# First stage of a graph recurrent kernel: each matmul of 500 columns issued as two of 250 columns

## The chip, the cores and the metric

The kernel runs on one core of a Trainium2 chip. The metric is the device time of one execution in microseconds. A core has a tensor engine (TensorE, "PE" in the profile, whose weight loads are listed apart as "PEld"), VectorE (DVE), ScalarE (ACT), GpSimd (POOL), and SyncE (SP), which here only issues DMAs. The engines run their own instruction streams and meet at semaphores.

## The reference, cut to what matters

With B = 2048 samples, N = 50 nodes, D = 32 features and T = 2 maskers, the part that the change touches is the first:

```
fusion = x.reshape(b, n * d)                                        # 2048 x 1600
adj = jnp.einsum('bn,tnm->btm', fusion, masker_param) + masker_bias # 2048 x 2 x 2500
adj = jax.nn.relu(adj).reshape(b, t, n, n)
adj = adj / (adj.sum(axis=-1, keepdims=True) + 1e-06)
```

After it come one graph recurrence step with adj (gates, sigmoid, tanh), a batch norm, a layer norm, attention scores with a softmax, and a weighted sum to the output of 2048 x 64.

## The kernel before, in words

Three stages run one after the other; only the first is changed. It computes adj, normalised and turned, and stores it to DRAM as adjT; the second stage (lines 674 to 716 on TensorE) does the recurrence, the third (lines 1149 to 1233) the norms and the attention.

In the first stage the product has the samples of a tile (128) as rows of the output, and the 5000 adjacency entries are cut into 10 groups of 500 columns (`GW`), each being 10 rows (`GN`) of 50. The outer loop goes over 2 blocks of 8 sample tiles, the next over the 10 groups, and the innermost over the 8 tiles of the block: 2 x 10 x 8 = 160 windows, numbered c. Even and odd windows (c2 = 0 and 1) use different buffers. The contraction of 1600 features (with the bias as a further row) takes 13 chunks of up to 128 rows.

Products are in the type fp32r. Each operand is split in a high part, its cast to fp32r, and a low part, the remainder (`x_hi`, `x_lo`, `w_hi`, `w_lo`), and three products (low x high, high x low, high x high) are added up in PSUM for each of the first 12 chunks; the last chunk needs two. So a window has 12 x 3 + 2 = 38 matmuls, the stationary operand being 128 columns of x, the moving one 500 columns of w, all accumulated into one PSUM bank (`mm_out(c2)`, bank 0 or 1). In the notation of the profile the second name of a row is the stationary operand: in "psum<-w_hi,x_lo" x_lo is loaded and w_hi streams.

In the middle of a window (after the chunks of unit `T_AT` = 3, so 24 matmuls in) TensorE does four transposes (line 321) of the window before, which wait for VectorE's `an_ready`. ScalarE does relu (line 229) from the finished bank into `u`, and later the copy of the transposed tile (line 235); VectorE does row sums, an addition, a reciprocal and a multiplication (lines 276 to 284) into `an`. At the last window of a group ScalarE and VectorE also split the next group's w (lines 210 and 216). A window's first matmul waits for `u_ready` of the window two before (its bank is then free). SyncE issues the loads of x and w and the store of each tile. PSUM has 8 banks of 512 fp32 a partition (`BANK` = 512); the first stage uses banks 0 and 1 for products, 2 and 3 for transposes.

Of the kernel before, what the change touches and what calls it, by code (L numbers as in the profile page):

```python
# [18 lines left out]
ACT = mybir.ActivationFunctionType  # L19
# [7 lines left out]
KF = KX // P  # L27
# [8 lines left out]
GW = GN * N  # L36
# [5 lines left out]
RK = 125  # L42
# [13 lines left out]
BANK = 512  # L56
# [27 lines left out]
def stage1(nc, psum, xT, W, adjT, ident_d):  # L84
    with ExitStack() as ctx:
# [9 lines left out]
        u = sb("u", [P, 2, GN, N])  # L95
# [8 lines left out]
        mm_done, u_ready, an_ready = sem("mm_done"), sem("u_ready"), sem("an_ready")  # L104
        tr_done, at_ready = sem("tr_done"), sem("at_ready")
        at_stored = [sem("at_stored0"), sem("at_stored1")]
        dve_step = sem("dve_step")

        def mm_out(c2):

            return psum[:, c2 * BANK:c2 * BANK + GW]

        def tr_out(c2):

            return psum[0:RK, (2 + c2) * BANK:(3 + c2) * BANK]

        block = ctx.enter_context(nc.Block())

# [55 lines left out]
        def split_x_hi(act, bt, half):  # L174
            act.wait_ge(x_loaded[half], 16 * (bt + 1))
            if bt >= BLK and half == 0:

                act.wait_ge(mm_done, (GROUPS - 1) * BLK + bt - BLK + 1)
            cols = bass.ts(bt % BLK, P)
            if half == 0:  # L180
                nc.scalar.copy(x_hi[:, 0:XH, cols], x_raw[:, 0:XH, :]).then_inc(x_hi_ready, 1)
            else:
                nc.scalar.copy(x_hi[:, XH:KF, cols], x_raw[:, XH:KF, :])
                nc.scalar.copy(x_hi[0:KLAST, KF, cols], x_raw[0:KLAST, KC, :])
                nc.scalar.copy(x_lo[:, KF, cols], x_raw[:, KF, :]).then_inc(x_hi_ready, 1)
# [12 lines left out]
        def split_w_hi(act, i, it):  # L198

            act.wait_ge(w_loaded[i], (it + 1) * 16)  # L200
            if not (isinstance(it, int) and it == 0):

                if i == NU - 1:
                    act.wait_ge(mm_done, it * BLK)
                else:
                    act.wait_ge(w_used, (it - 1) * (NU - 1) + i + 1)
            k0, k1 = UNITS[i]
            if i == NU - 1:
                nc.scalar.copy(w_lo[0:KLAST, KF, :], w_raw[0:KLAST, KC, :])
            nc.scalar.copy(w_hi[:, k0:k1, :], w_raw[:, k0:k1, :]).then_inc(w_hi_ready, 1)  # L210
# [12 lines left out]
        @block.scalar  # L223
        def _(act):
            def relu(c, c2, start=False):
                act.wait_ge(mm_done, c + 1)
                if not start:
                    act.wait_ge(an_ready, c - 1)
                nc.scalar.activation(u[:, c2].rearrange("p n m -> p (n m)"), mm_out(c2), ACT.Relu).then_inc(u_ready, 1)  # L229

            def evacuate(c, c2, start=False):
                act.wait_ge(tr_done, c + 1)
                if not start:
                    act.wait_ge(at_stored[c2], 8 * (c - c2))
                nc.scalar.copy(at[:, c2].rearrange("p k b -> p (k b)"), tr_out(c2)).then_inc(at_ready, 1)  # L235

            split_x_hi(act, 0, 0)
            for i in range(NU):
                split_w_hi(act, i, 0)
                if i == 0:  # L240
                    split_x_hi(act, 0, 1)
            for blk in range(BLOCKS):
                for it, group in p1_iters(act, blk):
                    static = isinstance(it, int)
                    for w in range(BLK):
                        c = it * BLK + w
                        split = w == BLK - 1 and not (static and it == ITERS - 1)
                        if not (static and it == 0 and w == 0):
                            relu(c - 1, (w - 1) % 2, start=static and it == 0 and w <= 2)
                        if static and it == GROUPS and w == 0:  # L250
                            for half in range(2):
                                split_x_hi(act, 2 * BLK - 1, half)
                        if static and it == 0 and w + 1 < BLK:
                            for half in range(2):
                                split_x_hi(act, w + 1, half)
                        if split:
                            for i in range(0, T_AT + 1):
                                split_w_hi(act, i, it + 1)
                        if not (static and it == 0 and w == 0):
                            evacuate(c - 1, (w - 1) % 2, start=static and it == 0 and w <= 2)  # L260
                        if split:
                            for i in range(T_AT + 1, NU):
                                split_w_hi(act, i, it + 1)
                        if static and it == GROUPS - 1 and w >= 1:
                            for half in range(2):
                                split_x_hi(act, BLK + w - 1, half)
            c = ITERS * BLK - 1
            relu(c, 1)
            evacuate(c, 1)

# [42 lines left out]
        @block.tensor  # L313
        def _(pe):
            def transposes(c, c2, start=False):
                pe.wait_ge(an_ready, c + 1)
                if not start:
                    pe.wait_ge(at_ready, c - 1)
                flat = an[:, c2].rearrange("p n m -> p (n m)")
                for k in range(AK):  # L320
                    last = nc.tensor.transpose(tr_out(c2)[:, k * P:(k + 1) * P], flat[:, k * RK:(k + 1) * RK], ident[:, :])  # L321
                last.then_inc(tr_done, 1)

            def window(it, w, blk, c, start=False, bank_free=False, none_before=False):
                pe.wait_ge(x_ready, 2 * (blk * BLK + w) + 1)
                if not bank_free:
                    pe.wait_ge(u_ready, c - 1)
                cols = bass.ts(w, P)
                for i, (k0, k1) in enumerate(UNITS):
                    if i == X_UNIT:  # L330
                        pe.wait_ge(x_ready, 2 * (blk * BLK + w) + 2)
                    if w == 0:
                        pe.wait_ge(w_ready, it * NU + i + 1)
                    for k in range(k0, k1):
                        if k < KF:
                            products = ((x_lo, w_hi, P), (x_hi, w_lo, P), (x_hi, w_hi, P))
                        else:
                            products = ((x_lo, w_hi, P), (x_hi, w_lo, KLAST))
                        for n, (a, b, r) in enumerate(products):
                            last = nc.tensor.matmul(mm_out(w % 2), a[0:r, k, cols], b[0:r, k, :],  # L340
                                                    start=k == 0 and n == 0, stop=k == KF and n == 1)
                    if i == NU - 1:
                        last.then_inc(mm_done, 1)
                    elif w == BLK - 1:
                        last.then_inc(w_used, 1)
                    if none_before and i == NU - 1:
                        pe.wait_ge(ident_loaded, 16)
                    if i == T_AT and not none_before:
                        transposes(c - 1, (w - 1) % 2, start=start)

            for blk in range(BLOCKS):
                for it, group in pe_iters(pe, blk):
                    static = isinstance(it, int)
                    for w in range(BLK):
                        c = it * BLK + w
                        window(it, w, blk, c, start=static and it == 0 and w <= 2,
                               bank_free=static and it == 0 and w < 2, none_before=static and it == 0 and w == 0)
            transposes(ITERS * BLK - 1, 1)

def p1_iters(eng, blk):

    base = blk * GROUPS
    yield base, 0
    with eng.Fori(1, GROUPS - 1) as g:
        yield base + g, g
    yield base + GROUPS - 1, GROUPS - 1

def pe_iters(eng, blk):  # L370

    base = blk * GROUPS
    if blk == 0:
        yield 0, 0
    with eng.Fori(1 if blk == 0 else 0, GROUPS) as g:
        yield base + g, g
# [979 lines left out]
```

## Time and profile before

| | |
|---|---|
| median of 2 runs | 2315.03 us (2314.99 to 2315.07) |
| profiled execution, its own time | 2318.24 us |
| its span, first to last instruction | 2316.5 us |
| mean granted TensorE clock | 0.973 of full speed |
| TensorE busy (matmuls) | 2198.9 us, 95% |
| weight loads busy | 1737.8 us, 75% |
| VectorE, ScalarE, GpSimd busy | 1091.0, 962.2 and 136.2 us |

The profiled execution is 1.74 us longer than its span and 3.21 us longer than the median of the runs. The busy time of overlapping matmuls is counted once, and a matmul's recorded length holds its passage through the array as well, so that consecutive ones overlap. What an instruction costs TensorE is therefore read from the distance between the starts of two neighbours, not from the length of one.

### The profile page before, as it was taken

To read this page: it belongs to the slowest core of one execution; us is meant where nothing else is said; L and a number is where in the kernel's file an instruction comes from. 1 tells how busy PE (TensorE), PEld (TensorE's weight loads), DVE (VectorE), ACT (ScalarE), POOL (GpSimd) and SP (SyncE) were. 2 spreads that over 40 slices of the span, in tenths; PEclk is the share of its full clock that TensorE was granted. 3 is DMA by queue.
4 is the path that set the end of the run, shared out by engine and by line. 5 is a ranking of instruction groups with operands and counts; after the bars stand their busy time and mean duration, and the time that the engine had idled before them with its cause. 6 is when DMAs were issued, how large, how long until landed. Compare 5 with 4: busy or idle time off the path is not lost. (4 is left out here: it accounts for less than half of the span.)

```text
span 2316.5 us, 34741 instructions
## 1 busy us (share of the span) xinstructions
PE 2198.9 (95%) x12302; PEld 1737.8 (75%) x12302; DVE 1091.0 (47%) x2177; ACT 962.2 (42%) x1637; POOL 136.2 (6%) x124
## 2 busy tenths in 40 slices
PE   8999999999999999999999999299999999975888
PEld 7888888888888888888888888277777777752333
DVE  4433233332345223333233332178888888873656
ACT  4322122221234212222122221088888988865551
POOL 0000000000000000000000000011101111104340
PEclk9999999999999999999999999699999999986899
DMA  6421222212234222221222211577777677619440
GB/s 208 151 75 44 88 91 90 74 45 88 92 128 143 64 90 90 91 69 50 89 90 91 72 48 27 124 171 184 186 201 181 188 199 181 181 65 261 122 119 5
DMA packets 341744, 264.06 MB, mean 114 GB/s; under 512 B 169334, under 2 KB 302998, under 8 KB 339990
## 3 DMA queue, kind: packets, MB, share of 16 engines
q1 hardware_dynamic: 323546, 225.69, 34.5%
q10 hardware_dynamic: 18144, 37.69, 5.0%
q8 instruction: 29, 0.48, 0.1%
q14 instruction: 25, 0.20, 0.0%
HBM read 195.65 MB, written 67.70 MB: 114 GB/s over the span
## 5 line engine op out<-in xcount | busy, mean ns | idle before, releaser
L340 PE MATMUL psum<-w_hi,x_lo 128*128 128x500 f32 x2080 | 823.0, 396 | 8.6 <-DVE w_lo L216 8.6
L340 PE MATMUL psum<-w_lo,x_hi 128*128 128x500 f32 (+1 forms) x2080 | 811.0, 390 | 0.0
L340 PE MATMUL psum<-w_hi,x_hi 128*128 128x500 f32 x1920 | 745.1, 388 | 0.0
L276 DVE TENSOR_REDUCE rows<-u 128x10 f32<-128x500 f32 x160 | 107.7, 673 | 893.5 <-ACT u L229 892.8
L340 PEld LDWEIGHTS psum<-w_hi,x_lo 128*128 128x128 f32 x2080 | 392.1, 188 | 84.4 <-issue 7.9
L340 PEld LDWEIGHTS psum<-w_lo,x_hi 128*128 128x128 f32 (+1 forms) x2080 | 392.5, 189 | 73.2
L340 PEld LDWEIGHTS psum<-w_hi,x_hi 128*128 128x128 f32 x1920 | 361.7, 188 | 72.9
L235 ACT COPY at<-psum 125x512 f32<-125x512 f32 x160 | 93.8, 586 | 677.4 <-PE psum L321 677.4
L229 ACT ACTIVATE u<-psum 128x500 f32<-128x500 f32 x160 | 94.1, 588 | 342.4 <-PE psum L340 342.3
L674 PE MATMUL psum<-adj_sb,xs_sb 100*64 100x100 f32 x2048 | 200.6, 350 | 30.1 <-DMA xs_sb<-xz 30.1
L674 PEld LDWEIGHTS psum<-adj_sb,xs_sb 100*64 100x64 f32 x2048 | 144.4, 149 | 73.9 <-issue 63.7
L652 POOL TENSOR_TENSOR xg_lo<-xg_sb,xg_hi 128x400 fp32r<-128x400 f32 x64 | 67.1, 1049 | 1961.4 <-ACT xg_hi L486 1961.4
L520 ACT ACTIVATE r_gate<-psum,bias 64x400 f32<-64x400 f32 x256 | 151.2, 591 | 18.3 <-PE psum L699 15.8
L216 DVE TENSOR_TENSOR w_lo<-w_raw,w_hi 128x1000 fp32r<-128x1000 f32 x120 | 144.1, 1201 | 23.6 <-ACT w_hi L210 17.4
L210 ACT CAST w_hi<-w_raw 128x1000 fp32r<-128x1000 f32 (+1 forms) x140 | 135.6, 969 | 46.3 <-PE psum L340 45.0
L525 ACT ACTIVATE psum<-psum,bias 64x400 f32<-64x400 f32 x256 | 142.3, 556 | 12.7 <-DVE hG L595 6.9
L284 DVE TENSOR_TENSOR an<-u,rows 128x500 f32<-128x500 f32 x160 | 108.8, 680 | 6.9
L603 DVE BATCH_NORM_STATS2 stats<-hC 128x128 f32 (+1 forms) x400 | 88.7, 282 | 49.3 <-ACT hC L498 48.9
L321 PEld LDWEIGHTS psum<-ident_sb,an 128*125 128x125 f32 x640 | 94.1, 186 | 17.8 <-DVE an L284 3.2
L321 PE MATMUL psum<-ident_sb,an 128*125 128x128 f32 x640 | 96.0, 272 | 4.0 <-DVE an L284 4.0
L1013 DVE SCALAR_TENSOR_TENSOR pr<-h,nmu_sb,psum 128x512 f32<-128x512 f32 x100 | 70.5, 743 | 47.0 <-PE psum L1221 24.6
L570 DVE TENSOR_TENSOR m_lo<-psum,m_hi 128x400 fp32r<-128x400 f32 x128 | 70.6, 552 | 28.6 <-ACT m_hi L490 28.6
(160 smaller groups left out, 2284.8 us busy)
## 6 DMA issues: line engine op xcount, KB each, us to landing
w_raw<-W SPq DMA_DIRECT2D x140, 500.0 KB, 7.9
adjT<-at SPq DMA_DIRECT2D x160, 250.0 KB
adj_sb<-adjT SPq DMA_DIRECT2D x32, 1250.0 KB
xs_sb<-xz SPq DMA_DIRECT2D x16, 1600.0 KB
hF<-hC ACTq DMA_DIRECT2D x96, 256.0 KB, 6.7
h<-hF SPq DMA_DIRECT2D x64, 256.0 KB, 4.5
xg_sb<-xg ACTq DMA_DIRECT2D x14, 800.0 KB, 8.0
h<-hF SPq DMA_DIRECT2D x48, 192.0 KB, 3.7
```

What stands on the lines that cost most here:

```text
L210: nc.scalar.copy(w_hi[:, k0:k1, :], w_raw[:, k0:k1, :]).then_inc(w_hi_ready, 1)
L216: nc.vector.tensor_tensor(w_lo[:, k0:k1, :], w_raw[:, k0:k1, :], w_hi[:, k0:k1, :].bitcast(fp32), ALU.subtract).then_inc(w_ready, 1)
L229: nc.scalar.activation(u[:, c2].rearrange("p n m -> p (n m)"), mm_out(c2), ACT.Relu).then_inc(u_ready, 1)
L235: nc.scalar.copy(at[:, c2].rearrange("p k b -> p (k b)"), tr_out(c2)).then_inc(at_ready, 1)
L276: nc.vector.tensor_reduce(rows[:, 0], u[:, c2], AX.X, ALU.add).then_inc(dve_step, 1)
L284: nc.vector.tensor_tensor(an[:, c2], u[:, c2], rows[:, 2].unsqueeze(2).to_broadcast([P, GN, N]), ALU.mult).then_inc(an_ready, 1)
L321: last = nc.tensor.transpose(tr_out(c2)[:, k * P:(k + 1) * P], flat[:, k * RK:(k + 1) * RK], ident[:, :])
L340: last = nc.tensor.matmul(mm_out(w % 2), a[0:r, k, cols], b[0:r, k, :], start=k == 0 and n == 0, stop=k == KF and n == 1)
L520: last = nc.scalar.activation(r_gate[half], rz_bank(pair)[half], ACT.Sigmoid, bias=bias[half, R_G:R_G + 1])
L525: last = nc.scalar.activation(z_bank[half], rz_bank(pair)[other], ACT.Sigmoid, bias=bias[other, Z_G:Z_G + 1])
L603: last = nc.vector.bn_stats(stats[:, bass.ds(tile, 1), c, :].rearrange("p i v -> p (i v)"), hC[:, c, :])
L674: last = nc.tensor.matmul(out_[SH * i:SH * i + SH, :, gi], xs[:, r, b, :], adj[:, r, :, b], start=True, stop=True)
```

## The change: two halves into two banks

Each of the 38 products of a window is issued as two matmuls with the same stationary operand, one for columns 0 to 249 and one for 250 to 499 of w. They write the first 250 columns of two neighbouring banks. `mm_out(c2)` becomes a view of both banks, `[P, 2, 250]`, and relu reads it in one instruction. Products take banks 0 to 3, transposes move to banks 4 and 5. The semaphores, their counts and the order of everything else are as before.

```diff
+        HW = GW // 2
+
+        def mm_half(c2, part):
+
+            return psum[:, (2 * c2 + part) * BANK:(2 * c2 + part) * BANK + HW]
+
         def mm_out(c2):
 
-            return psum[:, c2 * BANK:c2 * BANK + GW]
+            return psum[:, 2 * c2 * BANK:(2 * c2 + 2) * BANK].rearrange("p (h n) -> p h n", h=2)[:, :, 0:HW]
 
         def tr_out(c2):
 
-            return psum[0:RK, (2 + c2) * BANK:(3 + c2) * BANK]
+            return psum[0:RK, (4 + c2) * BANK:(5 + c2) * BANK]
...
-                nc.scalar.activation(u[:, c2].rearrange("p n m -> p (n m)"), mm_out(c2), ACT.Relu).then_inc(u_ready, 1)
+                nc.scalar.activation(u[:, c2].rearrange("p (h n) m -> p h (n m)", h=2), mm_out(c2), ACT.Relu).then_inc(u_ready, 1)
...
                         for n, (a, b, r) in enumerate(products):
-                            last = nc.tensor.matmul(mm_out(w % 2), a[0:r, k, cols], b[0:r, k, :],
-                                                    start=k == 0 and n == 0, stop=k == KF and n == 1)
+                            for part in range(2):
+                                last = nc.tensor.matmul(mm_half(w % 2, part), a[0:r, k, cols], b[0:r, k, part * HW:part * HW + HW],
+                                                        start=k == 0 and n == 0, stop=k == KF and n == 1)
```

## Rows read from the trace of the kernel before

**Rows 1.** The page: span, busy time of each engine, granted TensorE clock in 40 slices.

```profile
span 2316.5 us, 34741 instructions
PE 2198.9 (95%) x12302; PEld 1737.8 (75%) x12302; DVE 1091.0 (47%) x2177; ACT 962.2 (42%) x1637; POOL 136.2 (6%) x124
...
PEclk9999999999999999999999999699999999986899
```

**Rows 2.** Busy by stretch: length, PE, PEld, DVE, ACT, POOL, clock, DMA, GB/s.

```profile
300.00:500.00 200.00, 200.00 (x931) 167.73 (x930) 56.91 (x106) 42.77 (x64) 0.00 (x0) 1.00 0.25 82
...
1600.00:2000.00 400.00, 399.98 (x3389) 316.84 (x3386) 346.83 (x785) 354.81 (x673) 48.35 (x46) 1.00 0.73 189
```

**Rows 3.** The one line 229, relu: durations, first and last start, what it waits for.

```profile
L229 ACT ACTIVATE u<-psum x160: 576/588/592, 21.5 to 1460.1; 128x500 f32<-128x500 f32 x160
...
  PE psum L340: 342.3, 139
```

**Rows 4.** Timeline of one window: start, length (us), engine, line.

```profile
500.35 0.39 PE L340 MATMUL psum<-w_hi,x_lo 128*128 128x500 f32 x1
...
502.33 0.68 DVE L284 TENSOR_TENSOR an<-u,rows 128x500 f32<-128x500 f32 x1
...
505.52 0.39 PE L340 MATMUL psum<-w_hi,x_hi 128*128 128x500 f32 x1
505.75 0.60 PE L321 MATMUL psum<-ident_sb,an 128*125 128x128 f32 x4
...
506.11 0.48 PE L340 MATMUL psum<-w_hi,x_lo 128*128 128x500 f32 x1
...
506.42 0.39 PE L340 MATMUL psum<-w_lo,x_hi 128*128 128x500 f32 x1
```

**Rows 5.** The page, costliest groups, line 340: busy us, mean ns, idle before.

```profile
L340 PE MATMUL psum<-w_hi,x_lo 128*128 128x500 f32 x2080 | 823.0, 396 | 8.6 <-DVE w_lo L216 8.6
L340 PE MATMUL psum<-w_lo,x_hi 128*128 128x500 f32 (+1 forms) x2080 | 811.0, 390 | 0.0
L340 PE MATMUL psum<-w_hi,x_hi 128*128 128x500 f32 x1920 | 745.1, 388 | 0.0
...
L340 PEld LDWEIGHTS psum<-w_hi,x_lo 128*128 128x128 f32 x2080 | 392.1, 188 | 84.4 <-issue 7.9
L340 PEld LDWEIGHTS psum<-w_lo,x_hi 128*128 128x128 f32 (+1 forms) x2080 | 392.5, 189 | 73.2
L340 PEld LDWEIGHTS psum<-w_hi,x_hi 128*128 128x128 f32 x1920 | 361.7, 188 | 72.9
```

**Rows 6.** The one line 321, transposes: durations ns min/median/max.

```profile
L321 PE MATMUL psum<-ident_sb,an x640: 270/272/374, 26.7 to 1463.0; 128*125 128x128 f32 x160
```

**Rows 7.** Timeline of the third stage: loads and matmuls of 512 columns.

```profile
2211.23 0.19 PEld L1208 LDWEIGHTS psum<-w_lo,spread_sb 100*128 100x128 f32 x1 [0.84 <-issue]
...
2211.34 0.19 PEld L1209 LDWEIGHTS psum<-w_hi,spread_sb 100*128 100x128 f32 x1
...
2211.57 0.39 PE L1209 MATMUL psum<-w_hi,spread_sb 100*128 100x512 f32 x1
...
2211.81 0.39 PE L1208 MATMUL psum<-w_lo,spread_sb 100*128 100x512 f32 x1
...
2212.97 0.40 PE L1209 MATMUL psum<-w_hi,spread_sb 100*128 100x512 f32 x1
```

**Rows 8.** Timeline of the second stage: four intervals of 400 columns.

```profile
1962.14 0.34 PE L705 MATMUL psum<-m_lo,wd_hi 128*128 128x400 f32 x1
...
1962.87 0.35 PE L705 MATMUL psum<-xg_hi,wd_hi 128*128 128x400 f32 x1
```

**Rows 9.** Instructions of ScalarE by line and shape, first stage.

```profile
L181 ACT CAST x_hi<-x_raw 128x1024 fp32r<-128x1024 f32 x10 | 10.5, 1050 | 17.1 <-DMA x_raw<-xT 14.6 <-PE psum L340 2.6
...
L185 ACT CAST x_lo<-x_raw 128x128 fp32r<-128x128 f32 x10 | 3.0, 297 | 0.0
```

**Rows 10.** Timeline of the second stage: plain fp32 matmuls of 100 columns.

```profile
1963.15 1.57 PE L674 MATMUL psum<-adj_sb,xs_sb 100*64 100x100 f32 x16
```

## The prediction, made before the change was built

> **What bounds the kernel now.** I read the page first, for how full the engines are: the span is 2316.5 us, TensorE has matmuls in 95% of it, and its granted clock is full (2.4 GHz) in every slice of the first 1400 us [rows 1]. Busy time by stretch comes next, for where that is true: from 300 to 500 us TensorE is busy in 200.00 of 200.00 us, VectorE in 56.91 and ScalarE in 42.77 [rows 2]. The first stage is bound by TensorE alone, and the others have three quarters of their time free. Third, the group of relu: its 160 runs start between 21.5 and 1460.1 us, and ScalarE mostly waits for the product of line 340 before one (342.3 us in 139 waits) [rows 3]. So 159 windows take 1438.6 us, which is 9.048 us a window, and whatever a window costs TensorE more or less goes to the end time 160 times. The later stages are not touched; they start when the last tile is stored.
>
> Last, the timeline of one window, for what TensorE pays per instruction. The transposes take it from 505.75 to 506.11, 0.36 us, and the matmul after them 0.31 us where others take 0.225, 0.085 more [rows 4]. That leaves 9.048 - 0.445 = 8.603 us for 38 products: **226.4 ns for a load and 500 columns**. Taken directly from the timeline, 23 intervals between 500.35 and 505.52 make 224.8 ns [rows 4]; I use 226.4, since it holds all windows. 500 columns at 2.4 GHz are 208.3 ns, so 18.1 ns of each interval are something else. Whether these 18.1 ns belong to the instruction or to its columns decides this change.
>
> **The loads.** The change adds 160 x 38 = 6080 matmuls. Does the second half load its stationary again? The kernel before has this case: x_hi of a chunk multiplies w_lo and then w_hi, the same 128 columns twice in a row, and there are as many loads as matmuls in each group, 2080, 2080 and 1920 [rows 5]. So 6080 loads come with them. What does a load cost? Where the matmul is short, the load sets the pace: the four transposes (128 moving columns, 53 ns at 2.4 GHz, and a stationary of 125) take 0.60 us as a merged row [rows 4], one of them has a length of 272 ns [rows 6], so three intervals are 0.328 us, 109 ns each. The third stage shows it more directly for fp32r: after a pause the first load starts at 2211.23 and the second at 2211.34, 0.11 us, and from there the matmuls follow at their usual pace [rows 7]. I take 109 to 110 ns for an exposed load. A load runs beside the matmul ahead of it, so a half takes the larger of 109 and its own streaming: 250 columns are 104.2 ns, and the load alone is longer than that. The pair of halves is therefore no shorter than 2 x 109 = 218 ns. The cover that hides the loads today (107 to 110 ns under 226) becomes nearly as short as they are.
>
> **The streaming of 250 columns.** No fp32r matmul under 400 columns is in the trace. Three widths are: 400 columns take (1962.87 - 1962.14) / 4 = 182.5 ns [rows 8], 500 take 226.4, and 512 take (2212.97 - 2211.57) / 6 = 233.3 ns [rows 7], each with a load of 128 columns beside it. Over the pure columns (166.7, 208.3 and 213.3) these are 15.8, 18.1 and 20.0 ns.
> - If the surplus is per instruction (a load disturbs the stream once), 250 columns take 104.2 + 18.1 = 122.3, a pair 244.6: +18.2 ns.
> - If it is per column, 0.4528 ns each, 250 columns take 113.2 and a pair 226.4: nothing.
> - The surplus grows with the width, though not from nothing at every fit: the line through 400 and 500 (0.439 ns a column) gives 116.6 at 250, the least-squares line through all three (0.448) 115.2.
>
> The nearest evidence is these three widths, and 250 is far off them, with the load's length now as long as the stream's. I take 116 ns, near the upper of the two lines, because any unevenness of two things that are equally long adds: a pair of 232 ns, **+5.6 ns for each of 6080 products, +34 us**. The ends are 218 (-8.4 ns, -51 us) and 244.6 (+111 us).
>
> The Trainium skill ("TensorE: Matmul & The Clock Gate", Back-to-back issue gap) puts the start-to-start distance at the columns over 2.4 GHz plus a fixed 2.5 ns. The trace disagrees with the sum, 226.4 where the page would have 210.8. Only the fixed part would double here; that is the second rival below.
>
> **The rest, part by part.**
> - Two banks for a window: the third stage changes its bank between 2211.57 and 2211.81 and the mean of six intervals, half of them within one bank, is 233.3 [rows 7], so alternating banks costs or gives back at most some 5 ns an interval in rounded starts. I take nothing.
> - Relu over two banks is one instruction of 588 ns before [rows 3]. Casts of 1024 and 128 elements take 1050 and 297 ns [rows 9], 0.84 ns an element and 190 ns fixed; at worst the second bank costs one fixed part, at best nothing. Either is hidden: `an` starts at 502.33 and ends 503.01, and the transposes that need it start at 505.75 [rows 4], 2.7 us later, which 0.19 us more does not touch. Queued behind relu on ScalarE are the copy of line 235 and the w splits, with ScalarE a fifth busy. Uncovered it would be at most 0.19 us, once, at the stage's last window.
> - The waits on `u_ready` (bank free) are for two windows before, 18 us back, and stay met. `mm_done` comes with the second half, a tenth of a microsecond after the first: nothing. `w_used` the same. No DMA, queue order or semaphore count is changed, SyncE's and GpSimd's queues neither.
> - Issue: TensorE's instruction stream must deliver a load and a matmul every 116 ns. In the second stage 3389 matmuls were delivered in 400 us, 118 ns each [rows 2], as the sustained rate of a mix. It shows that 118 is possible; that the stream could do 116 is not shown. I charge nothing and let it speak for the upper side.
>
> **Sum.** Against the profiled execution: 2316.5 + 34 = 2350.5 us of span, 2352.3 with the 1.7 us around it. The median lies 3.2 us under its profiled execution; the forecast for it is 2315 + 34 = 2349, and I put 2350.
>
> **Rivals.**
> - *The surplus is per instruction.* For: a load runs beside every matmul and both read operands; the surplus at 400 and 500 columns differs by only 2.3 of 18.1 ns. Against: a purely fixed part would make no such difference. Each product +18.2 ns, 6080 x 18.2 = +111 us, 2426 us, slower. It decides as soon as a half takes more than 117.0 ns, where the 2% lie (+46 us is 7.6 ns a product).
> - *The columns cost what they cost.* The surplus is all per column but for a small fixed part. For: 0.456, 0.453 and 0.456 ns a column at the three widths, which is nearly one constant. Against: the load then becomes almost as long as the stream. At 113.2 to 114.5 ns a half it gives 2315 to 2331. By the page's fixed 2.5 ns, an estimate, it would be +15 us.
> - *The load is the whole pace.* Short streams lose their surplus because it was contention in a long stream, and halves run at 109 ns: 2315 - 51 = 2264, faster by 2.2%. For: the transposes do exactly that. Against: 104.2 ns of columns are twice those of a transpose, and any surplus over 5 ns breaks it.
> - *A short fp32r matmul doesn't keep its rate*, or the load is no longer hidden. Plain fp32 matmuls of 100 columns run two at a time, 16 in 1.57 us, so two take up to 0.196 us, 1.96 ns a column [rows 10]. At that pace a half takes 490 ns and the kernel some 6900 us; with load and stream one after the other (109 + 104) a product takes 427 and the kernel 3530. Nothing in the trace points to either.
> - *The change does not do what it says*: if the second half needed no load, as the counts exclude, a product would be one stream of 500 columns as before, no change; its chance is in that of the constant column price.
>
> **How the numbers follow.** The forecast (halves between 114.6 and 117.5 ns, 2332 to 2367) 0.42; the fixed surplus and what lies between, 2367 to 2430, 0.32; the constant column price 0.15; the load as pace 0.05; far slower 0.06. The range takes the first three: 2312 to 2430, with the two lines' own 2332 to 2367 as the forecast's range. Two per cent, about what a measurement of this kernel tells from no change, is 46 us: slower than 2361 are the second and last case and a sixth of the first, 0.45; faster 0.05; within 0.50.
>
> **What would show it.** In the profile after: 12160 matmuls of 128x250 and 12160 loads at the product's line (if loads stay at 6080, the first part is wrong); the mean distance of starts in the first stage near 116 ns (122 for the fixed surplus, 113 for the column price, 109 for the load's pace); starts of loads as far apart as those of matmuls; weight loads busy nearly all of the first stage; 9.26 us a window between relus; the second and third stage as long as before; relu between 588 and 780 ns with no new waiter. The prediction fails if a half takes under 112 or over 123 ns, or if "issue" ends TensorE's idle time in the first stage.

## The result and the profile after

The changed kernel takes 2363.07 us, the median of two runs (2361.76 and 2364.39), against 2315.03: 1.0208 times as long, 95% interval 1.0164 to 1.0251. Run again beside others it took 2361.80 us, 1.0200 times (1.0179 to 1.0220). The forecast was 2350 us, its range 2312 to 2430.

The page of the changed kernel, its first lines, the granted clock and the costliest groups; these answer to [rows 1] and [rows 5]:

```profile
span 2360.0 us, 46901 instructions
PE 2246.3 (95%) x18382; PEld 2017.6 (85%) x18382; DVE 1091.1 (46%) x2177; ACT 962.1 (41%) x1637; POOL 136.3 (6%) x124
...
PEclk9999999999999999999999999789999999986999
...
L347 PE MATMUL psum<-w_hi,x_lo 128*128 128x250 f32 x4160 | 840.4, 283 | 8.1 <-DVE w_lo L222 8.1
L347 PE MATMUL psum<-w_lo,x_hi 128*128 128x250 f32 (+1 forms) x4160 | 824.7, 279 | 0.0
L347 PE MATMUL psum<-w_hi,x_hi 128*128 128x250 f32 x3840 | 760.8, 280 | 0.0
L347 PEld LDWEIGHTS psum<-w_hi,x_lo 128*128 128x128 f32 x4160 | 637.7, 190 | 8.1 <-issue 8.1
L347 PEld LDWEIGHTS psum<-w_lo,x_hi 128*128 128x128 f32 (+1 forms) x4160 | 640.2, 190 | 0.0
L347 PEld LDWEIGHTS psum<-w_hi,x_hi 128*128 128x128 f32 x3840 | 589.6, 190 | 0.0
```

There are 12160 matmuls at the product's line now (4160 + 4160 + 3840) and 12160 loads, so the second half does load its stationary again. Matmuls are TensorE's busy time in the same 95% of a longer span; what fills up is the weight load, from 1737.8 to 2017.6 us. The clock row is nearly as before. In the groups the idle time in front of the weight loads has gone from 84.4, 73.2 and 72.9 us to 8.1, 0 and 0: before, every load had a pause before it. Busy time of the first stage by stretch (length, matmuls, loads, VectorE, ScalarE, GpSimd, clock, DMA share, GB/s), against [rows 2], says the same:

```profile
300.00:500.00 200.00, 200.00 (x1716) 200.00 (x1715) 60.84 (x109) 45.70 (x66) 0.00 (x0) 1.00 0.25 81
```

Loads are in flight 200.00 us of 200.00, as the matmuls are. Recorded lengths of loads overlap each other and their own pace is shorter, so this alone is not proof that they are the limit. The one line of relu, its durations, the first and last start and what it waits for, against [rows 3]:

```profile
L235 ACT ACTIVATE u<-psum x160: 577/590/591, 18.7 to 1504.9; 128x500 f32<-128x500 f32 x160
...
  PE psum L347: 357.3, 140
```

Relu from two banks takes 590 ns at the median, from one it took 588. The 159 windows take 1504.9 - 18.7 = 1486.2 us, 9.347 us each, 0.299 more than the 9.048 before; 160 windows make 47.9 us, and the medians are 48.0 apart. So the whole loss is in the first stage's windows. The spans of the two profiled executions are only 43.5 us apart (2360.0 and 2316.5): of the 47.6 us between the first and the last relu, 2.8 are taken off since relu starts earlier in this one (18.7 us, not 21.5; the trace's first rise of the clock lies at 11.2 us, not 16.8), and 1.3 since what follows the last relu is that much shorter. The timeline of one (start, length, merged neighbours of the same form), against [rows 4]:

```profile
500.26 0.60 PE L327 MATMUL psum<-ident_sb,an 128*125 128x128 f32 x4
500.62 0.48 PE L347 MATMUL psum<-w_hi,x_lo 128*128 128x250 f32 x2
500.94 0.40 PE L347 MATMUL psum<-w_lo,x_hi 128*128 128x250 f32 x2
501.18 0.39 PE L347 MATMUL psum<-w_hi,x_hi 128*128 128x250 f32 x2
...
502.81 0.40 PE L347 MATMUL psum<-w_hi,x_lo 128*128 128x250 f32 x2
```

The four transposes take 0.36 us as before, and the first product behind them 0.32 where others take 0.235: the same 0.085 more. Seven products from 501.18 to 502.81 take 1.63 us. With the window's 9.347 - 0.445 = 8.902 us over 38 products, **a product takes 234.3 ns, a half 117.1**, where 232 and 116 were forecast and 226.4 was the product before.

### The profile page after: what moved, and what is told of

Its sections match the earlier page's. It is cut to its first block and busy times, and to the rows that moved or that the text cites. A ratio compares the mean times of both kernels' runs of the same rounds, so it can differ in the third digit from the quotient of the medians.

```text
span 2360.0 us, 46901 instructions
## 1 busy us (share of the span) xinstructions
PE 2246.3 (95%) x18382; PEld 2017.6 (85%) x18382; DVE 1091.1 (46%) x2177; ACT 962.1 (41%) x1637; POOL 136.3 (6%) x124
## 5 line engine op out<-in xcount | busy, mean ns | idle before, releaser
L347 PE MATMUL psum<-w_hi,x_lo 128*128 128x250 f32 x4160 | 840.4, 283 | 8.1 <-DVE w_lo L222 8.1
L347 PE MATMUL psum<-w_lo,x_hi 128*128 128x250 f32 (+1 forms) x4160 | 824.7, 279 | 0.0
L347 PE MATMUL psum<-w_hi,x_hi 128*128 128x250 f32 x3840 | 760.8, 280 | 0.0
L347 PEld LDWEIGHTS psum<-w_hi,x_lo 128*128 128x128 f32 x4160 | 637.7, 190 | 8.1 <-issue 8.1
L347 PEld LDWEIGHTS psum<-w_lo,x_hi 128*128 128x128 f32 (+1 forms) x4160 | 640.2, 190 | 0.0
L347 PEld LDWEIGHTS psum<-w_hi,x_hi 128*128 128x128 f32 x3840 | 589.6, 190 | 0.0
L681 PEld LDWEIGHTS psum<-adj_sb,xs_sb 100*64 100x64 f32 x2048 | 144.4, 149 | 73.2 <-issue 63.0
L327 PEld LDWEIGHTS psum<-ident_sb,an 128*125 128x125 f32 x640 | 83.6, 187 | 4.1 <-DVE an L290 2.8
```

The source lines that it names most:

```text
L347: last = nc.tensor.matmul(mm_half(w % 2, part), a[0:r, k, cols], b[0:r, k, part * HW:part * HW + HW], start=k == 0 and n == 0, stop=k == K ...
L681: last = nc.tensor.matmul(out_[SH * i:SH * i + SH, :, gi], xs[:, r, b, :], adj[:, r, :, b], start=True, stop=True)
```

## The experiments

The distances told below are between starts of neighbouring matmuls. Where "medians" are given, the median over the 159 windows was taken for each place in the window, and the places with the same width were averaged; places beside the transposes are left out. Places with the same width are not alike: their medians run from 220 to 232 ns in the kernel before and from 111 to 124 in the changed one. A mean of five or six places is therefore good to about 1 ns, an estimate from this scatter (2.5 to 3 ns for one place). A window's time, over 36 or 38 products in 159 windows, is the safer figure.

**The two banks.** The halves of 36 products go into one bank; `mm_out`, the transposes' banks and relu are those of the kernel before, from which this differs by:

```diff
+        HW = GW // 2
...
-                            last = nc.tensor.matmul(mm_out(w % 2), a[0:r, k, cols], b[0:r, k, :],
-                                                    start=k == 0 and n == 0, stop=k == KF and n == 1)
+                            whole = (k == 0 and n == 0) or (k == KF and n == 1)
+                            for part in range(1 if whole else 2):
+                                q = slice(0, GW) if whole else slice(part * HW, part * HW + HW)
+                                last = nc.tensor.matmul(mm_out(w % 2)[:, q], a[0:r, k, cols], b[0:r, k, q],
+                                                        start=k == 0 and n == 0, stop=k == KF and n == 1)
```

> The halves of 36 of the 38 products of a window go into one bank, as columns 0 to 249 and 250 to 499; the first and the last product stay whole. The changed kernel's halves start 117.2 ns apart, a product 234.3. If the bank plays no part (my theory), the same here: 36 products by +8 ns in each of 160 windows, +46 us on 2315, so 2359 to 2363 us. If changing the bank at every matmul costs something, the distance falls to 113 or less and the time is under 2330; if it helps, over 2375.

Measured: 2357.43 us, 1.0181 (1.0164 to 1.0198). Its relu:

```profile
L231 ACT ACTIVATE u<-psum x160: 574/588/590, 18.7 to 1502.0; 128x500 f32<-128x500 f32 x160
```

A window is (1502.0 - 18.7) / 159 = 9.329 us. Less 0.445 and two whole products of 0.2264 it leaves 8.431 us for 36, 234.2 ns a product, as with two banks. The time is 1.6 us under the expected 2359 to 2363, far from the 2330 or 2375 that a price of the bank would have given. The bank plays no part.

**The same stationary twice.** The changed kernel, but per chunk all products of the first half, then all of the second:

```diff
-                        for n, (a, b, r) in enumerate(products):
-                            for part in range(2):
+                        for part in range(2):
+                            for n, (a, b, r) in enumerate(products):
```

> Within a chunk all products of the first half go before all of the second, so that no two neighbours have the same stationary except w_lo and w_hi under x_hi. In the changed kernel the first half starts 116 ns before the second and the second 118.5 ns before the next product. If loading the same columns again is what makes the first distance shorter, all distances become 118 to 119 and the time is up by 5 to 15 us on 2363. If it is the place of the columns in w, or chance, the mean stays at 117 and the time at 2363 within 3 us: my theory.

Measured: 2360.32 us, 1.0204 (1.0187 to 1.0221). Its relu:

```profile
L235 ACT ACTIVATE u<-psum x160: 577/590/590, 19.2 to 1505.7; 128x500 f32<-128x500 f32 x160
```

A window of 9.349 us, as in the changed kernel. Loading the same columns again is neither cheaper nor dearer than loading others. By medians the two halves are 116.5 and 117.8 ns here, where the changed kernel has 115.5 and 118.2: what one half gains in the order the other loses, and only the sum is a price.

**Distance against width.** The kernel before with one matmul a product, of many widths; the rest of the columns is left out:

```diff
+WIDTHS = (500, 400, 300, 250, 200, 128, 500)
...
+                            width = WIDTHS[k // 2]
+                            last = nc.tensor.matmul(mm_out(w % 2)[:, 0:width], a[0:r, k, cols], b[0:r, k, 0:width],
```

> Not the whole product: in each window the chunks stream 500, 400, 300, 250, 200, 128 and 500 columns (two chunks each), the rest of the columns is left out. Distances of starts by width, with 128 columns loaded each time. Surplus per column (0.453 to 0.469 ns a column, never under the load's 109): 226, 182, 137, 115, 109, 109. Surplus per instruction of 13 to 18 ns: 226, 183, 141, 120, 109, 109. Load as the pace with an unevenness when both are nearly equal (my theory): 226, 182, 138, 117, 110, 109, with 250 above the line through 400 and 300.

Measured: 1941.17 us. The timeline of a window; the distance is read from the first of a width to the first of the next:

```profile
402.19 0.39 PE L343 MATMUL psum<-w_hi,x_lo 128*128 128x500 f32 x1
...
403.56 0.34 PE L343 MATMUL psum<-w_hi,x_lo 128*128 128x400 f32 x1
...
404.66 0.30 PE L343 MATMUL psum<-w_hi,x_lo 128*128 128x300 f32 x1
...
405.49 0.28 PE L343 MATMUL psum<-w_hi,x_lo 128*128 128x250 f32 x1
...
406.07 0.28 PE L343 MATMUL psum<-w_hi,x_hi 128*128 128x250 f32 x1
...
406.72 0.28 PE L343 MATMUL psum<-w_lo,x_hi 128*128 128x200 f32 x1
...
407.28 0.24 PE L343 MATMUL psum<-w_hi,x_lo 128*128 128x128 f32 x1
407.35 0.28 PE L343 MATMUL psum<-w_lo,x_hi 128*128 128x128 f32 x1
...
407.91 0.44 PE L343 MATMUL psum<-w_hi,x_lo 128*128 128x500 f32 x1
```

From 402.19 to 403.56 are six intervals of 500 columns, 228 ns each; 400 columns 183, 300 columns 138; 250 columns from 405.49 to 406.07 (five) 116, 200 columns 112, and 128 columns, from 407.35 to 407.91, 112. The medians are 226.5, 182.3, 138.0, 117.0, 112.0 and 112.0 ns. Where the width changes, the recorded starts shift: the first place of 128 columns shows 77 ns and the first of 500 behind them 282; these two are left out. Under 250 columns the distance stops falling: there the load sets the pace, at 112 ns, somewhat more than the 109 of the transposes.

The same with loads of 64 columns of x:

```diff
+                            m = P if (k == 0 and n == 0) or k == KF else P // 2
...
+                            last = nc.tensor.matmul(mm_out(w % 2)[0:m, 0:width], a[0:r, k, w * P:w * P + m], b[0:r, k, 0:width],
```

> As the run of many widths, but all products except the first of a window and those of the last chunk load only 64 of the 128 columns of x, half of the samples being left out. If the surplus comes from the load running beside the stream, it halves: 500, 400, 300, 250, 200 and 128 columns at 217, 174, 132, 111, 90 and 60 ns. If it belongs to the stream itself (my theory at 400 and 500), 226, 182, 137, 114, 92 and 60. At 250 the load of 53 ns is no limit, so a distance still near 117 would clear the load of the last nanoseconds, one near 113 would convict it.

Measured: 1891.55 us. The timeline of a window:

```profile
400.08 0.35 PE L344 MATMUL psum<-w_hi,x_lo 128*64 128x400 f32 x1
...
401.17 0.30 PE L344 MATMUL psum<-w_hi,x_lo 128*64 128x300 f32 x1
...
401.99 0.28 PE L344 MATMUL psum<-w_hi,x_lo 128*64 128x250 f32 x1
...
402.56 0.27 PE L344 MATMUL psum<-w_hi,x_hi 128*64 128x250 f32 x1
...
403.21 0.25 PE L344 MATMUL psum<-w_lo,x_hi 128*64 128x200 f32 x1
...
403.66 0.22 PE L344 MATMUL psum<-w_hi,x_lo 128*64 128x128 f32 x1
...
404.02 0.44 PE L344 MATMUL psum<-w_hi,x_lo 128*128 128x500 f32 x1
```

Here 400 columns take 182 ns, 300 take 137, 250 (401.99 to 402.56) 114, 200 (403.21 to 403.66) 90, and 128, from 403.66, 60. The medians are 225.0, 181.5, 136.2, 115.0, 91.2 and 59.7 ns. Without the load's floor the price is nearly a straight line: from 128 and 400 columns it is **0.448 ns a column and 2.4 ns an instruction**, and that line gives 226.4 at 500, 114.4 at 250 and 92.0 at 200. A least-squares line through all six has 0.445 and 2.8, so the fixed part is known to about half a nanosecond at best. The surplus of 18.1 ns at 500 columns is thus 2.4 ns of instruction and 15.7 of columns, and halving the load doesn't halve it. That ends the rival of a surplus per instruction: it would have had 128 columns at 71 ns.

The Trainium skill ("TensorE: Matmul & The Clock Gate", Back-to-back issue gap) has, for a matmul by itself, a gap of the columns over 2.4 GHz plus a fixed 2.5 ns. This trace agrees with the fixed part (2.4 to 2.8), not with the columns: the formula has 0.417 ns each, these runs show 0.448. For a stream of loads and matmuls, which is what this kernel is, the same section has 81 ns at 128 columns and 131 at 512; here a load and 128 columns take 112 and a load and 500 columns 226.

**The load's share, in place.** The changed kernel with loads of 64 columns (except a window's first product and last chunk), half of the samples left out:

```diff
+                            m = P if (k == 0 and n == 0) or k == KF else P // 2
...
-                                last = nc.tensor.matmul(mm_half(w % 2, part), a[0:r, k, cols], b[0:r, k, part * HW:part * HW + HW],
+                                last = nc.tensor.matmul(mm_half(w % 2, part)[0:m], a[0:r, k, w * P:w * P + m], b[0:r, k, part * HW:part * HW + HW],
```

> The changed kernel with 64 instead of 128 columns of x loaded for every matmul except those of a window's first product and last chunk, so half the samples are left out. The run of many widths gave 117.4 ns at 250 columns with loads of 128 and 114.8 with loads of 64. If the load that is nearly as long as the stream costs the last 2.6 ns of each half, 35 of 38 products are 5.2 ns shorter than in the changed kernel: 29 us, so 2331 to 2336 us, or 0.7% over the kernel before. If the load's length plays no part, 2361 to 2364.

Measured: 2351.63 us, 1.0163 (1.0143 to 1.0182). Its relu:

```profile
L235 ACT ACTIVATE u<-psum x160: 577/588/589, 18.7 to 1494.6; 128x500 f32<-128x500 f32 x160
```

The window is 9.282 us, 65 ns less than the changed kernel's, over 35 products 1.9 ns each. With the load halved about a quarter of the 7.9 ns goes, not the 5.2 ns that I expected: halves in the whole kernel are dearer than the single matmuls of the run of widths, with short loads too.

**Another cut.** The changed kernel cut at column 300, with relu as two instructions:

```diff
-        HW = GW // 2
+        CUT = 300
...
-                                last = nc.tensor.matmul(mm_half(w % 2, part), a[0:r, k, cols], b[0:r, k, part * HW:part * HW + HW],
+                                last = nc.tensor.matmul(mm_half(w % 2, part), a[0:r, k, cols], b[0:r, k, CUT:GW] if part else b[0:r, k, 0:CUT],
```

> The whole product, cut at column 300 instead of 250, relu as two instructions. If a matmul's distance is the larger of the load's pace and the columns' price (138 at 300, 113 at 200 in the run of many widths), a product takes 251 ns against 226.4 before: +148 us on 2315, 2463 us. If only columns counted, a product would stay near 228 and the time near 2325; if a fixed surplus of 18 ns an instruction, 245 and 2426.

Measured: 2454.12 us, 1.0602 (1.0582 to 1.0622). The timeline merges the two parts of a product:

```profile
500.08 0.41 PE L349 MATMUL psum<-w_hi,x_lo 128*128 128x300 f32 x2
...
501.82 0.41 PE L349 MATMUL psum<-w_lo,x_hi 128*128 128x300 f32 x2
```

Seven products in 1.74 us are 249 ns each: 138 for 300 columns and 112 for 200, from the run of widths, make 250. Loads alone would need 224 (2 x 112), columns alone 229. So the larger of load and columns is paid for each matmul, and a short one can't lend its spare time to a long one. The single starts don't show the two terms: by medians they lie 158 ns apart behind the 300 columns and 92 behind the 200, those of the loads 108 and 141. As at the changes of width above, a recorded start is not exact by itself, and the sum is the price.

**The changed kernel again:**

> The changed kernel once more, for a narrower interval beside the others: 2360 to 2365 us, 1.019 to 1.022 times the kernel before. Every theory expects this.

Measured: 2361.80 us, as told above.

**Four parts.** The kernel before with 36 products cut in 126, 124, 126 and 124 columns of one bank:

```diff
+                            whole = (k == 0 and n == 0) or (k == KF and n == 1)
+                            for q in (slice(0, GW),) if whole else (slice(0, 126), slice(126, 250), slice(250, 376), slice(376, 500)):
+                                last = nc.tensor.matmul(mm_out(w % 2)[:, q], a[0:r, k, cols], b[0:r, k, q],
```

> 36 of 38 products cut in four matmuls of 124 or 126 columns in one bank, the first and last whole. The load's pace of 111 to 112 ns decides alone: a cut product takes 446 ns, +220 on 226.4, for 5760 products +1265 us, so 3580 us. Columns alone would be 56 ns each and no change; a fixed surplus of 18 ns an instruction with hidden loads +54 ns a product, 2626 us.

Measured: 6055.52 us, 2.5 ms more than I expected. The timeline of a window in the first stage:

```profile
995.51 1.06 PE L342 MATMUL psum<-w_lo,x_hi 128*128 128x126 f32 x4
996.36 1.06 PE L342 MATMUL psum<-w_hi,x_hi 128*128 128x126 f32 x4
...
1012.24 0.62 PE L342 MATMUL psum<-w_hi,x_lo 128*128 128x500 f32 x1
1012.66 0.73 PE L342 MATMUL psum<-w_lo,x_hi 128*128 128x126 f32 x3
```

A cut product, four matmuls, takes 0.85 us, 213 ns each, and a whole one of 500 columns 0.42. These are nearly twice the 112 and 226 ns above, as at the 1.2 GHz level. The kernel before shows that level at its start: 500 columns take 0.42 us at 16 us and 0.22 at 17.

```profile
15.78 0.62 PE L340 MATMUL psum<-w_lo,x_hi 128*128 128x500 f32 x1
16.20 0.62 PE L340 MATMUL psum<-w_hi,x_hi 128*128 128x500 f32 x1
...
17.16 0.39 PE L340 MATMUL psum<-w_hi,x_hi 128*128 128x500 f32 x1
17.38 0.39 PE L340 MATMUL psum<-w_hi,x_lo 128*128 128x500 f32 x1
```

In the run of four parts the first stage never leaves it: over 5100 us, each matmul and each transpose has nearly twice its distance. 5760 products by (4 x 213 - 226.4) ns are 3603 us, and the rest (320 whole products and the transposes, at twice their price) some 0.13 ms: 6050. The granted clock on the page doesn't tell it:

```profile
PEclk9999999999999999999999999999999999999979
```

```profile
5194.00:5240.00 46.00, 5.27 (x41) 4.48 (x42) 6.53 (x32) 4.27 (x9) 4.06 (x4) 1.00 0.61 144
...
1464.00:1508.00 44.00, 5.90 (x46) 5.06 (x46) 5.35 (x29) 4.59 (x8) 4.06 (x4) 0.50 0.69 158
```

The kernel before has a recorded fall at 1464.0 us and reads 0.50; the run of four parts has no record yet and reads 1.00 for the same work. So ahead of the first recorded change the row tells nothing, and the distances are to be believed.

**Three parts** of 168, 168 and 164 columns, otherwise the same:

```diff
+                            for q in (slice(0, GW),) if whole else (slice(0, 168), slice(168, 336), slice(336, 500)):
```

> 36 of 38 products cut in three matmuls of 168, 168 and 164 columns in one bank. With quarters every distance was twice that of the others (213 ns for a load, 420 for 500 columns), as at the 1.2 GHz level, through the whole first stage. Here columns are 70 of each 112 ns. If the clock stays at 2.4 GHz, the load's pace of 112 decides: +110 ns for 5760 products, 2950 us. If it falls back to 1.2 GHz as with quarters, a cut product takes 3 x 213 = 639 ns and the kernel about 4800 us. I think the first likelier, since 200 and 128 columns went at 111 to 113 ns in the run of many widths.

Measured: 4821.50 us, the second of the two expectations. Its timeline, first stage:

```profile
1001.33 0.84 PE L342 MATMUL psum<-w_hi,x_hi 128*128 128x168 f32 x3
...
1005.17 0.84 PE L342 MATMUL psum<-w_hi,x_hi 128*128 128x168 f32 x3
```

Six products in 3.84 us are 640 ns, 3 x 213. The first recorded change of the clock is again a rise in the second stage, at 4013.3 us. Cut in three, then, TensorE stays at 1.2 GHz for the whole first stage; cut in two, it rises at 11.2 us. Why it doesn't rise is not shown: in the run of widths 200 and 128 columns were among longer ones, and went at full clock. What a product in three or four parts takes at 2.4 GHz wasn't measured.

**Cut at 252,** the changed kernel with relu as two instructions; otherwise as the cut at 300:

```diff
-        HW = GW // 2
+        CUT = 252
```

> The whole product cut at column 252, so that the second part starts 1008 bytes into the 2000 of a chunk, a multiple of 16, instead of 1000, which is not; relu as two instructions. In the changed kernel the first half takes 115.7 ns and the second 118.4. If the second is slower because its stream starts off a 16-byte boundary, it comes down to 115.5, -2.8 ns for 6080 products or -17 us: 2345 us. If it has to do with being the second (the load that follows is of other columns), nothing changes but two columns moved: 2362 us.

Measured: 2341.52 us, 1.0123 (1.0105 to 1.0140). Its second relu:

```profile
L237 ACT ACTIVATE u<-psum x160: 361/372/373, 19.4 to 1486.9; 128x248 f32<-128x248 f32 x160
```

A window is (1486.9 - 19.4) / 159 = 9.230 us, a product 231.2 ns, 3.1 less than when cut at 250. Two columns moved take back 20 of the 48 us. By medians the parts take 116.7 and 114.6 ns, where the halves of the changed kernel take 115.5 and 118.2: the second part is the one that has become cheaper. My reason, the second start on a 16-byte boundary, was put to two more runs.

**Starts and pieces.** In the kernel before, one matmul of a product is kept, with loads of 64 and many starts, then with loads of 128 and the pieces of both cuts:

```diff
+STARTS = (0, 250, 248, 1, 2, 4)
...
+                            m, at0, width = (P, 0, GW) if ends else (P // 2, STARTS[k // 2], 250)
```

> Not the whole product: one matmul of 250 columns a product with loads of 64, and the columns of w streamed from start 0, 250, 248, 1, 2 and 4 (two chunks each), that is at 0, 1000, 992, 4, 8 and 16 bytes. If the start's alignment to 16 bytes costs 3 ns: 114.5, 117.5, 114.5, 117.5, 117.5, 114.5 ns. If it costs nothing and the slower half is slow for another reason: all 114 to 115.

Measured: 1859.54 us. The medians are 115.4, 115.8, 115.5, 116.6, 116.0 and 115.8 ns. They lie within 1.2 ns, which is about what a mean of so few places is good to, so no start is shown to cost anything.

```diff
+PIECES = ((0, 250), (250, 250), (0, 252), (252, 248), (248, 252), (0, 248))
...
+                            at0, width = (0, GW) if ends else PIECES[k // 2]
```

> Not the whole product: one matmul a product with loads of 128, streaming (start, width) = (0, 250), (250, 250), (0, 252), (252, 248), (248, 252), (0, 248), two chunks each. If a start off a 16-byte boundary costs only beside a full load, (250, 250) takes 118.4 ns and the other pieces 114.5 to 116.5. If the width counts in steps of four columns (1.8 ns each), 116.5, 116.5, 116.5, 114.7, 116.5, 114.7. If the slower second half of the changed kernel comes from the load of the same columns before it, none of these shows 118.4.

Measured: 1857.62 us. The medians are 115.8, 116.3, 116.5, 115.6, 116.4 and 113.5 ns. (250, 250) costs 0.5 ns more than (0, 250), not 2.8, so my reason falls: by itself the boundary doesn't slow a second half beside a full load either. Widths that count in steps of four would have both pieces of 248 at 1.8 ns under the others; one is 3.0 under (0, 252), the other 0.8 under (248, 252), which is no clear answer. The pieces of the cut at 250 add up to 232.1, and those of the cut at 252 too; in the whole kernels it is 234.3 and 231.2. What makes the cut at 250 some 2 ns a product dearer in place than its pieces stays open. None of the runs that compute the whole product beats the kernel before.

## Why the prediction was right, point by point

- *What bounds the kernel:* right. The loss is 160 windows by 0.299 us, and nothing behind the last relu moved by more than 1.3 us. The clock, though, was not full in all of the first 1400 us: for the first 16.8 it was at 1.2 GHz, which the row doesn't show.
- *6080 loads come with the matmuls:* right, from the equal counts in [rows 5]. In which order they come makes no difference.
- *An exposed load is 109 to 110 ns:* a little short. At full clock short fp32r matmuls go at 112.
- *A half takes 116 ns:* the mis-sized term. It takes 117.1, and 2.3 ns a product in 6080 products are the 14 us between forecast and result (2350 and 2363). The forecast was put between two straight lines through 400, 500 and 512 columns, and the runs show in part what is in it. The line through the widths with short loads makes two halves dearer than a whole by its 2.4 ns; the full load beside the halves adds 1.9 (2361.80 us, against 2351.63 with half of it); that leaves 3.6 of 7.9. Moving the cut by two columns takes away 3.1, for a reason that stays open, and that these 3.1 are part of the 3.6 is argued, not shown. For "any unevenness of two things that are equally long adds" there is a price for the long load, a quarter of the sum; that unevenness makes it is not shown.
- *Luck:* the prediction has no term for the place of the cut. It would have put a cut at 252 at the same 2350 us, and that one measured 2341.52. That 2350 came as near as 13 us is therefore in part luck.
- *The range of the two lines:* 2332 to 2367 is called their own, but the lines, at 115.2 and 116.6 ns a half, give 2339 to 2356; the wider one is that of halves between 114.6 and 117.5.
- *Banks, relu, waits, issue:* nothing, as said. The bank was tried alone; relu takes 2 ns more and is covered; no idle time of TensorE's matmuls is put down to issue, though it gets a load and a matmul every 117 ns. The 8.1 us "issue" in front of the loads are one pause in the first 60 us, in which the matmuls wait for VectorE's w_lo, and the kernel before has 7.9 of them.
- *The rivals.* The surplus per instruction fell with the widths (60 ns at 128 columns). The constant column price, with its small fixed part, came nearest to the truth about the columns (0.448 ns and 2.4 fixed), but left out the load and the cut. The load's pace of 109 would have needed streams without surplus. "Far slower" was thought of as a loss of rate of short fp32r matmuls; the halves kept their rate. Thirds and quarters did run far slower, by a mechanism that the prediction did not have, the clock.

## What to carry to other kernels

Before splitting a matmul, read the pace at which loads go from the shortest matmuls in the trace and compare it with the column time of the parts: each matmul pays the larger of the two, each by itself (a little more where they are nearly equal, 117 ns for 112 and 114), and what is lost by going under is not given back by a longer neighbour (300 + 200 columns cost 23 ns more than 500, 250 + 250 cost 8). Splitting gained nothing here, even where the load is just covered; moving the cut by two columns was worth two fifths of the loss (20 of 48 us), and only a run told. Shorter parts can cost much more than their loads: here a first stage in parts of 124 to 168 columns stayed at 1.2 GHz, for a reason that is not shown. Ahead of the first recorded change of the clock this is read from the distance of starts, not from the clock's row.

## What the runs showed of the hardware that was not expected

- A first stage of which each matmul streams 124 to 168 columns beside loads of 128 ran at the 1.2 GHz level throughout (213 ns a matmul, 0.42 us for 500 columns, transposes too), in two kernels of 6055 and 4821 us; with 250 columns each it ran at 2.4 GHz.
- The page's granted clock showed the full level all that time, as it does in the first 16 us of the kernel before, where 500 columns take 0.42 us. The first change that these traces record is the rise at the end of it (5240.3, 4013.3 and 16.8 us).
- The column price of fp32r at 2.4 GHz is 0.448 ns, 7.5% over 1 / 2.4 GHz (from 128 and 400 columns with loads of 64; with loads of 128 the same from 250 columns up, within 2.6 ns).
- The cut of 500 columns at 252 costs 3.1 ns less than at 250, and neither the starts nor the pieces alone show why.
